# A Macaron block on one core: the FFN's gate columns put behind the first expert's weights, and that expert's product made a slot ahead

## What is computed

```python
logits = _l2norm(x, -1) @ _l2norm(sim_matrix, 0) - jax.nn.sigmoid(gates)
...
w = probs * (mask > 0)                              # (tokens, 16)
def mix(proj):
    pe = jnp.einsum('nc,ech->neh', x, proj)
    return jnp.einsum('ne,neh->nh', w, pe).reshape(B, T, H)
q, k, v = (mix(q_proj), mix(k_proj), mix(v_proj))   # H = 128
...
ao = jnp.einsum('bqk,bkh->bqh', attn, v).reshape(B * T, H)
wa = jnp.einsum('ne,nh->enh', w, ao)
out = jnp.einsum('enh,ehc->nc', wa, o_proj)
```

## Time and profile before

| | |
|---|---|
| median of 3 runs | 2987.8 us (2984.71 to 2990.12) |
| profiled execution, its own time | 2985.56 us |
| span of its records | 2983.8 us |
| TensorE busy | 2823.2 us, 95% of the span |
| VectorE / ScalarE / GpSimd busy | 2211.6 / 974.6 / 533.1 us |
| mean granted TensorE clock | 0.983 |
| FFN 1, attention, FFN 2 | about 0 to 860, 860 to 2142, 2142 to 2984 us |

### The profile page before, as it was taken

One profiled execution on the slowest core, in us unless ns is written; L12 is line 12 of the kernel. 1 busy time (PEld: TensorE's weight loads), 2 busy tenths in 40 slices (PEclk: granted clock), 3 DMA queues, 4 the chain that ended last, 5 costly groups with the idle time before them and its releaser, 6 DMA issues. The chain is left out here.

```text
span 2983.8 us, 54554 instructions
## 1 busy us (share of the span) xinstructions
PE 2823.2 (95%) x16740; PEld 2540.8 (85%) x16740; DVE 2211.6 (74%) x5934; ACT 974.6 (33%) x2688; POOL 533.1 (18%) x1432
## 2 busy tenths in 40 slices
PE   6999999999949999999999999999899999999998
PEld 5999999999938888887878787888689999999997
DVE  5888888888856767676767676766688888888887
ACT  3111111110026666565656565666521111111110
POOL 3233323333210000000000000000133333233231
PEclk8999999999979999999999999999899999999999
DMA  5000000000020000000000000000210000000000
GB/s 170 1 1 1 0 1 1 1 0 1 1 71 1 1 1 1 2 1 2 1 2 1 2 1 2 1 1 1 59 55 8 0 8 7 7 0 8 7 3 12
DMA packets 42882, 33.36 MB, mean 11 GB/s; under 512 B 2688, under 2 KB 41600, under 8 KB 42624
## 3 DMA queue, kind: packets, MB, share of 16 engines
q1 hardware_dynamic: 42624, 30.44, 3.3%
HBM read 26.24 MB, written 4.19 MB: 10 GB/s over the span
## 5 line engine op out<-in xcount | busy, mean ns | idle before, releaser
L448 PE MATMUL ffn_ring<-ffn_mix_weights,ffn_yT 128*128 128x384 f32 x6144 | 1249.5, 345 | 27.6 <-DVE ffn_mix_sums L613 11.5
L448 PEld LDWEIGHTS ffn_ring<-ffn_mix_weights,ffn_yT 128*128 128x128 f32 x6144 | 1084.9, 191 | 76.2 <-DVE ffn_mix_sums L613 16.8
L615 DVE SCALAR_TENSOR_TENSOR ffn_mix_sums<-ffn_ring,ffn_w,ffn_mix_sums 128x384 f32<-128x384 f32 x896 | 549.8, 615 | 203.9 <-PE ffn_ring L448 189.4
L499 PE MATMUL ffn_ring<-ffn_out_weights,ffn_avT 128*128 128x512 f32 x1536 | 439.0, 396 | 3.5 <-POOL ffn_avT L907 3.5
L1319 DVE TENSOR_REDUCE attn_score_neg_max<-attn_scores 128x1 f32<-128x512 f32 (+3 forms) x512 | 247.0, 482 | 242.4 <-PE attn_scores L1204 241.7
L1171 PE MATMUL attn_scores<-attn_kT,attn_qT 128*128 128x256 f32 (+2 forms) x1536 | 345.3, 333 | 12.3 <-issue 10.8
L499 PEld LDWEIGHTS ffn_ring<-ffn_out_weights,ffn_avT 128*128 128x128 f32 x1536 | 281.7, 188 | 29.0 <-POOL ffn_avT L907 4.7
L1423 ACT ACTIVATE attn_exponentials<-attn_scores,attn_score_neg_max 128x512 f32<-128x512 f32 (+3 forms) x512 | 269.6, 527 | 108.3 <-DVE attn_score_neg_max L1319 102.2
L630 DVE SCALAR_TENSOR_TENSOR x<-ffn_ring,ffn_w_out,x 128x256 f32 (+1 forms) x512 | 247.7, 484 | 52.4 <-PE ffn_ring L499 20.2
L1171 PE MATMUL attn_ctx<-attn_probsT,attn_v 128*128 128x256 f32 (+2 forms) x1536 | 275.7, 328 | 4.6 <-DVE attn_probsT L1339 4.0
L1339 DVE TENSOR_TENSOR attn_probsT<-attn_turned,attn_probsT 128x512 fp32r<-128x512 f32 (+3 forms) x512 | 248.0, 485 | 36.9 <-ACT attn_probsT L1438 36.6
(11 more groups left out here) (136 smaller groups left out, 3099.7 us busy)
## 6 DMA issues: line engine op xcount, KB each, us to landing
ffn_mix_stage<-in_L_ffn_q_proj_dram SPq DMA_DIRECT2D x32, 128.0 KB, 2.6
ffn_mix_stage<-in_L_ffn_k_proj_dram SPq DMA_DIRECT2D x32, 128.0 KB, 2.6
ffn_mix_stage<-in_L_ffn_v_proj_dram SPq DMA_DIRECT2D x32, 128.0 KB, 2.9
ffn_out_stage<-in_L_ffn_o_proj_dram SPq DMA_DIRECT2D x16, 256.0 KB, 3.4
out_dram<-x SPq DMA_DIRECT2D x8, 512.0 KB, 3.3
x<-in_L_attn_x_dram SPq DMA_DIRECT2D x7, 512.0 KB, 7.8
attn_weight_stage<-in_L_attn_w_q_dram SPq DMA_DIRECT2D x4, 512.0 KB, 7.7
attn_weight_stage<-in_L_attn_w_dense_dram SPq DMA_DIRECT2D x4, 512.0 KB, 9.8
```

Source lines behind the costliest of these rows:

```text
L448: last = pe.matmul(bank[:, 0:QKV], yT[:, t % 2, h, k * P:(k + 1) * P], wm[:, e, wh, k], start=(n == 0), stop=(n == 3 * CK - 1))
L499: last = pe.matmul(bank[:], avT[:, t % 2, h], wo[:, g, wh], start=(i == 0), stop=(i == 2))
L615: dve.scalar_tensor_tensor(into, bank[:, 0:QKV], w[:, t, e:e + 1], into, ALU.mult, ALU.add).then_inc(mix_done, 1)
```

## The change

Three things in `ffn`:

- The weights' buffer `wm` is laid out anew. The high half of expert 0 gets rows of `WIDE` = 384 + 32 columns, and its last 32 are the gate columns, copied from `m.simw` by ScalarE once at each FFN's start (`sim_in`). The six matmuls of expert 0 are now four of 416 columns (with the high weights) and two of 384, and columns 384 to 415 of the product are the gate dots. `gate_dots` is gone.
- Expert 0 leaves the ring and gets an eighth PSUM bank of its own, `head`. Its product for tile T+1 is made in slot T, at the place where the gate dots were (`mix_first`, behind the third expert). In slot 0, tile 0's product comes first, ahead of the loop of experts. The ring keeps its numbering, with place 0 empty.
- VectorE reads dots and expert 0 from `head`. `mix_ready` now counts 15 experts a tile. `scores` no longer waits for `dot_read`.

`AHEAD` is 3 in both versions.

```diff
+WIDE = QKV + 2 * E
...
-        wm = sb("mix_weights", [P, E, 2, CK, QKV], F32R)
+        wm = sb("mix_weights", [P, CK * WIDE + (2 * E - 1) * CK * QKV], F32R)
...
+        head = ps("first_expert")
...
-                p = i - RING
+                p = i - RING if i != RING or not inside(T, 0) else -RING
...
-            def gate_dots(T, t):
-
+            def mix_first(T, t):
 
                 pe.wait_ge(yT_hi, T + 1)
                 pe.wait_ge(yT_lo, T + 1)
-                if const and isinstance(T, int) and T == 0:
-                    pe.wait_ge(const.lo, 1)
-                reach(pe, dot_read, T)
+                if isinstance(T, int) and T == 0:
+                    pe.wait_ge(sim_in, 1)
+                    split_done(pe, 0)
+                reach(pe, mix_done, E * (T - 1) + 1)
+                n = 0
                 for k in range(CK):
-                    for half in range(2):
-                        last = pe.matmul(sc[:, 0:2 * E], yT[:, t % 2, half, k * P:(k + 1) * P], m.simw[:, k],
-                                         start=(k == 0 and half == 0), stop=(k == CK - 1 and half == 1))
-                last.then_inc(dots_ready, 1)
+                    for h, wh in ((0, 0), (0, 1), (1, 0)):
+                        moving = mix_half(0, 1)[:, k] if wh else gate_columns(slice(0, WIDE))[:, k]
+                        width = QKV if wh else WIDE
+                        last = pe.matmul(head[:, 0:width], yT[:, t % 2, h, k * P:(k + 1) * P], moving,
+                                         start=(n == 0), stop=(n == 3 * CK - 1))
+                        n += 1
+                last.then_inc(head_ready, 1)
...
-                pe.wait_ge(dot_read, (T + 3) if inside(T + 2, 0) else TILES)
...
-                    if inside(T, 0):
+                    if inside(T, 0) and e > 0:
                         mix(T, t, e)
-                    if isinstance(T, int) and T == 0 and e == 0:
-                        gate_dots(0, 0)
...
                     if e == 2 and inside(T, -1):
-                        gate_dots(T + 1, (t + 1) % QT)
+                        mix_first(T + 1, (t + 1) % QT)
...
             transpose_y(0, 0)
+            mix_first(0, 0)
...
-                dve.wait_ge(dots_ready, T + 1)
-                dve.tensor_copy(dot[:], sc[:, E:2 * E]).then_inc(logit_done, 1)
+                dve.wait_ge(head_ready, T + 1)
+                dve.tensor_copy(dot[:], head[:, QKV + E:WIDE]).then_inc(logit_done, 1)
...
-                bank = ring[mix_bank(T, e)]
+                bank = ring[mix_bank(T, e)] if e else head
...
-                dve.wait_ge(mix_ready, E * T + e + 1)
+                if e:
+                    dve.wait_ge(mix_ready, (E - 1) * T + e)
+                else:
+                    dve.wait_ge(head_ready, T + 1)
...
                 const.split_hi(act)
+                act.wait_ge(const.lo, 1)
+            act.activation(gate_columns(slice(QKV, WIDE)), as_f32(m.simw[:]), ACT.Copy).then_inc(sim_in, 1)
             split_weights(0)
```

## The result

| | before | after |
|---|---|---|
| median of 15 runs each, same chip | 2987.6 us (2984.6 to 2990.1) | 2994.2 us (2989.9 to 3000.2) |
| ratio | 1 | 1.0022, 95% interval 1.0015 to 1.0030 |
| profiled execution, its own time | 2985.56 us | 2996.45 us |
| span | 2983.8 us | 2994.6 us |
| mean granted TensorE clock | 0.983 | 0.977 |

The changed kernel is 6.6 us slower, where 2.3 us faster was forecast. 2994.2 lies within the range of 2975 to 2995, but only just. The profiled execution of the changed kernel lies 2.3 us above its median, so the spans differ by 10.8 us and the medians by 6.6.

The account below looks back on a forecast made before the run. TensorE was taken as the bound, busy 2823.2 of 2983.8 us. Per FFN, +1.4, -0.4, -4.7, +3.5 and -0.9 came together to -1.1, for two FFNs -2.3: 2985.5 us, range 2975 to about 2995.

Parts of the forecast that it names:

- the loop's top: Slots behind the FFN loop's jump: TensorE's wait grows from 1.1 to 2.1 us, slot +0.575 us, 6 returns an FFN.
- The gate matmuls: Four 32-column matmuls per tile: removal saves 0.44 us, wider first-expert columns cost 0.055, net -0.385 us per tile on TensorE.
- The pause that stays (3008): Rival: the 0.36 us is a pause behind the third expert that remains without the small matmuls; 3008 us, chance 0.03.
- The ordinary slot: FFN slots away from the loop's jump: -0.385 plus a new wait of 0.17, -0.215 us each, 22 an FFN.
- The short wait: TensorE's third expert waits for expert 0's sum in each ordinary slot: about 0.17 us, bounds 0 and 0.27.
- The gap at the top: VectorE's jump between L598 and L613 at the FFN loop's top: 12 times, 27.3 us in all, taken to stay.
- The starts: First slots of each FFN: slot 0 +1.4 us, slot 1 0; bounds 0 and 1.4 for each FFN.
- The last slot: Slot 31 of each FFN, without gate matmuls before or a first expert made after: -0.9 us.
- Attention: The attention stage was taken as untouched by the change.
- the short wait isn't seen: Rival: no new wait at the third expert; 44 slots by 0.17, 7.5 us more off, 2978 us, chance 0.12.
- the whole saving arrives: Rival: expert 0's sum comes early enough everywhere; 60 by 0.385, 23 us off, 2965 us, chance 0.08.
- VectorE's gap grows: Rival: VectorE's longer loop body lengthens its gap at the jump; 2989 us in proportion, 3013 if doubled, chance 0.13.

Follow-up runs that it names:

- the runs with filler: Changed kernel with 8 or 4 useless extra matmuls ahead of the third expert in the loop's first slot (t = 2): 2987.3 us with 8, 2986.9 us with 4.
- the closed ring: Changed kernel with the ring's empty place 0 removed, 23 places a slot, so banks turn by one from slot to slot: 2966.1 us, ratio 0.9933.
- the reordered kernel: Kernel before, with two VectorE operations moved ahead of the first expert's sum in the loop's first slot (t = 2): 2992.8 us, ratio 1.0021.
- the flat kernel before: Kernel before with the loop over slots 2 to 29 written out in both FFNs, no jumps: 2970.8 us, ratio 0.9942.
- the flat changed kernel: Changed kernel with the loop over slots 2 to 29 written out in both FFNs: 2967.0 us, ratio 0.9935.
- the flat ring: Changed kernel with 23 ring places, the first expert's product moved behind the fourth expert, and slots 2 to 29 written out: 2955.5 us, ratio 0.9887.

## Why the prediction was wrong, point by point

**The step that failed** is the loop's top. The prediction said "The wait itself doubles, from 1.1 to 2.1 us", priced the return at +0.575, and stopped there. Both numbers came true: 1.9 us idle, and +0.62 at the 4 returns with the full clock, at all 12 in the runs with filler (0.59 to 0.65). What it did not ask is what TensorE does after a wait of that length: at 8 of 12 returns it goes on at half the clock and loses 1.56 us more. Where filler takes the falls away, and less the filler's own cost in slot 2, the kernel is at 2984.6 or 2985.7, that is 4.0 and 2.4 us under the kernel before on the same chip, against a forecast of 2.3. The prediction looked at the clock only for the price of slot 0 and named no rival in which it moved. Its reading that TensorE has no gap at a jump holds for the FFN's loop alone: at attention's five returns, in the same trace, TensorE stands 1.94 to 2.31 us, and the half clock behind three of them was there to be read.

**The gate matmuls** were worth what the rows said: 0.45 a tile removed, 0.40 net of the wider columns, against 0.44 and 0.385. The pause that stays (3008) is ruled out. The Trainium skill ("TensorE: Matmul & The Clock Gate", Wait — 56ns, not 53.3ns?) states about 25 ns as the least distance between small matmuls; the 0.09 of this trace (0.36 for four) lies above it, and a price of 0.10 for the four is ruled out.

**The ordinary slot** came out at -0.19 and not -0.215, inside a pass at -0.16. The short wait is real and 0.24 long (the 0.40 of the closed ring less 0.16). The prediction took 0.17, because it gave the spared wait instruction 0.08 to 0.09 from a slot outside the loop; in ordinary slots of the loop it brought 0.02 to 0.03, and only at the returns 0.09. Its bound of 0.27 ("if the spared instruction brings nothing") was the nearer one. The 44 slots bring 8.3 us and not 9.5.

**The gap at the top** did not grow with the body (27.3 to 26.2 us), as forecast. Slot 2 was right (-0.36, forecast -0.4).

**The starts** were priced at +1.4 an FFN with bounds of 0 and 1.4. Four traces of the changed kernel, with and without filler, give -0.1 to +3.4 an FFN, mean 1.4. That the mean meets the forecast is luck: it is 0.1 in slot 0, which was priced, and 1.3 in slot 1, which was taken as covered. And the reordered kernel, whose starts are those of before, has +2.7 in FFN 2 when the 1.0 of its own reordering is taken off. So this term is not told from what traces differ by, and the bounds were too narrow.

**The last slot** was priced at -0.9 an FFN. From the last sum of expert 0 in FFN 2 to the end, the changed kernel's two traces are 1.0 and 1.1 shorter than the one before; kernels that don't touch this slot are up to 1.4 shorter and the filled ones 0.5 longer. So no run shows this term either.

**Attention** was taken as untouched. The stretch from slot 31 of FFN 1 to slot 0 of FFN 2 lies between 6.0 under and 1.6 over that of the kernel before in the other ten traces with loops in the FFNs. That is as much as the change.

**The rivals**: that the short wait isn't seen, and that the whole saving arrives, are both ruled out by the slots. That VectorE's gap grows is ruled out by its 26.2 us. The kernel ended on the slower side by a mechanism that none of them held.

## What to carry to other kernels

When a change makes TensorE wait longer, the wait can have a price of its own beyond its length: look in the trace before, in every stage, for waits of the new length and for the clock behind them. Here attention's returns had both. When a product leaves a ring of buffers, close the ring up: the empty place kept a wait alive that took more than half of the saving in each slot (0.24 of 0.40). A few matmuls of nothing in a wait are a quick test of whether the clock is at fault.

## What was unexpected of the hardware

- In the FFNs' loops an idle time of 1.87 to 2.17 us, between stretches at full load, was followed by a granted clock of half in 19 of 36 returns, one of 1.5 or less in none, and the places moved between executions of one kernel. Each fall cost 1.5 to 1.6 us. At attention's returns it was 39 of 52 with 1.75 to 2.46 us of idle time. The Trainium skill ("TensorE: Matmul & The Clock Gate", A second HAM failure mode: psum-queue depth-cycling) describes swings of the clock in a kernel whose matmul groups are parted by frequent short idle times. The traces agree that idle times this short bring the clock down; here a single one does it, at returns some 100 us apart.
- Straight code instead of loops in the FFNs made attention's own loop slower: its stretch is 4.6 us longer than in the looped kernel before for the flat kernel before, 12.6 for the flat changed kernel and 14.2 for the flat ring, where the looped traces lie between -6.0 and +1.6. TensorE in the flat changed kernel, behind a return to attention's loop:

```profile
1182.41 0.50 PE L1228 MATMUL attn_turned<-ident,attn_probs 128*128 128x128 f32 x3
1184.38 0.37 PE L1228 MATMUL attn_turned<-ident,attn_probs 128*128 128x128 f32 x1 [1.47 <-issue]
```

In the kernel before, and in its flat version, these four stand together. Here TensorE stops in the middle of the group, waiting for nothing that the profile shows, at all five returns (1.3 to 1.7 us), and the half clock behind this return lasts 10 us; in the kernel before it is 3 us, or none. The Trainium skill ("Runtime: NRT & Kernel Launch", Instruction fetch mechanics) says that kernels prefer full unrolling where possible, because a jump breaks the fetching of instructions ahead. For VectorE in the FFN the traces agree (a step of 2.46 us at a return is 0.37 in straight code); but a loop that remains was slower here beside straight code. Why, and whether it is the place of its code, was not tried.
